# A perceiver block on one core: K and V of all heads first, queries by seven block products, and self scores on 64x64 tiles

## What is computed

```python
def _L0_xattn_ref(q, k, v, Wq, Wk, Wv, Wd):
    queries = (q @ Wq.T).reshape(B, Sq, NHEADS, HEAD_DIM).transpose(0, 2, 1, 3)
    keys = (k @ Wk.T).reshape(B, Skv, KVHEADS, HEAD_DIM).transpose(0, 2, 1, 3)
    values = (v @ Wv.T).reshape(B, Skv, KVHEADS, HEAD_DIM).transpose(0, 2, 1, 3)
    queries = _rope(queries)
    keys = _rope(keys)
    ...
    scores = jnp.einsum('bhqd,bhkd->bhqk', queries, keys) * scale
    scores = jnp.where(causal[None, None], scores, jnp.finfo(scores.dtype).min)
    attn = jax.nn.softmax(scores, axis=-1)
    ctx = jnp.einsum('bhqk,bhkd->bhqd', attn, values)
    ctx = ctx.transpose(0, 2, 1, 3).reshape(B, Sq, NHEADS * HEAD_DIM)
    return ctx @ Wd.T
...
x = x + _L0_xattn_ref(_layernorm(x, axis=-1), ctx_4096, ctx_4096, ...)
x = x + _L0_attn_ref(_layernorm(x, axis=-1), ...)
x = x + _L0_ffn_ref(x, ...)
```

## Time and profile before

| | |
|---|---|
| time, median of 3 runs | 783.68 us (783.64 to 783.75) |
| the profiled execution | 783.46 us, span 781.6 us, the remaining 1.9 us lie outside the span |
| mean granted TensorE clock | 0.985 of full speed |
| first projection matmul | 9.10 us after the span's start |
| first cross scores | 42.49 us |
| last LN transposes ahead of the self attention | 591.48 us |
| end | 781.6 us |

### The profile page before, as it was taken

The page is one execution under the profiler, slowest core; times in us unless marked ns, Lnnn a source line. Parts: engine busy times, 40 slices in busy tenths (PEclk is TensorE's granted clock), DMA queues, the critical chain, the costliest instruction groups (busy, mean ns, idle before and its releaser), DMA issues.

```text
span 781.6 us, 12794 instructions
## 1 busy us (share of the span) xinstructions
PE 757.0 (97%) x4624; PEld 615.4 (79%) x4624; DVE 509.9 (65%) x927; ACT 388.7 (50%) x692; POOL 468.3 (60%) x363
## 2 busy tenths in 40 slices
PE   6989999999999999999999999999799999999898
PEld 4768888888888888888888888888578777777786
DVE  6876565656656565664665656557677777788855
ACT  3557437454553744556274365545436665663220
POOL 4548646764863874686386467646354788864450
PEclk9799999999999999999999999999799999999999
DMA  8102101200210120030021012002002010010002
GB/s 304 55 2 81 55 0 54 81 0 0 85 49 0 55 79 0 24 110 0 0 81 54 0 54 81 0 1 80 3 1 81 14 55 1 2 57 26 14 1 108
DMA packets 11339, 34.11 MB, mean 44 GB/s; under 512 B 1456, under 2 KB 1584, under 8 KB 11312
## 3 DMA queue, kind: packets, MB, share of 16 engines
q1 hardware_dynamic: 11312, 33.75, 13.0%
HBM read 31.65 MB, written 2.10 MB: 43 GB/s over the span
## 4 chain that ended last, share of the span: by engine, by line
PE 86%; DVE 6%; issue 3%; ACT 2%; POOL 2%; DMA 1%; SPq 0%; POOLq 0%; DVEq 0%; ACTq 0%
PE pj L1110 53%; PE pj L1262 8%; PE sc L1142 4%; PE sc L1307 4%; PE pv L1331 2%; PE tp L1320 2%; PE pv L1157 2%; PE pv L1158 2%; PE tp L1150 2%; DVE sm L755 2%; PE pj L1403 1%; PE pj L1466 1%; PE tp L1134 1%; PE pv L1466 1%; PE tp L1466 1%
## 5 line engine op out<-in xcount | busy, mean ns | idle before, releaser
L398 POOL TENSOR_TENSOR sw<-sw,cst 128x512 f32<-128x512 f32 x79 | 109.3, 1383 | 60.7 <-ACT sw L539 60.7
L410 POOL TENSOR_TENSOR sm<-sm,mx 128x512 f32<-128x512 f32 x64 | 67.3, 1051 | 117.8 <-DVE mx L790 117.8
L563 ACT ACTIVATE sm<-sm 128x512 f32<-128x512 f32 x64 | 40.4, 632 | 140.0 <-POOL sm L410 139.7
L538 ACT ACTIVATE sw<-pj 64x512 f32<-64x512 f32 x80 | 47.6, 596 | 118.1 <-DVE t L780 117.7
L1110 PE MATMUL pj<-xh,wqh 128*128 128x512 f32 x252 | 103.4, 410 | 0.2 <-ACT sw L539 0.2
L1110 PE MATMUL pj<-wdh,ch 128*128 128x512 f32 x256 | 101.8, 398 | 0.7 <-ACT sw L539 0.5
L1110 PE MATMUL pj<-wdh,cl 128*128 128x512 f32 x256 | 99.7, 390 | 0.0
L1110 PE MATMUL pj<-wdl,ch 128*128 128x512 f32 x256 | 99.7, 390 | 0.0
L415 POOL TENSOR_TENSOR sm<-sm,rz 128x512 f32<-128x512 f32 x64 | 66.8, 1044 | 54.9 <-DVE rz L797 54.9
L1110 PE MATMUL pj<-xh,wql 128*128 128x512 f32 x252 | 99.7, 395 | 0.0
L1110 PE MATMUL pj<-xl,wqh 128*128 128x512 f32 x252 | 99.3, 394 | 0.0
(11 more groups left out here) (201 smaller groups left out, 1727.7 us busy)
## 6 DMA issues: line engine op xcount, KB each, us to landing
raw<-in_w_x SPq DMA_DIRECT2D x40, 512.0 KB, 3.9
qr<-in_ctxT SPq DMA_DIRECT2D x4, 512.0 KB, 7.1
X<-in_x SPq DMA_DIRECT2D x4, 512.0 KB, 7.3
raw<-in_w_s SPq DMA_DIRECT2D x4, 512.0 KB, 3.6
out<-X SPq DMA_DIRECT2D x8, 256.0 KB, 2.1
raw<-in_w_s SPq DMA_DIRECT2D x4, 256.0 KB, 3.0
raw<-in_w_o SPq DMA_DIRECT2D x2, 512.0 KB, 3.6
raw<-in_w_b SPq DMA_DIRECT2D x2, 512.0 KB, 4.8
```

Of the source, the lines that this page charges most:

```text
L398: pool.tensor_tensor(sw[par][:, :].rearrange("p (b s) -> p b s", s=S), sw[par][:, :].rearrange("p (b s) -> p b s", s=S), rep(cst[:, C_SIN: ...
L410: pool.tensor_tensor(s3, s3, per_group(mx[:, c, :], 8), ALU.subtract).then_inc(subbed, 1)
L538: act.activation(sw[par][0:64, :], src[64:128, :], ACT.Copy)
```

## The change

**K and V first.** All 16 K tiles (`k_tile`, 8 heads by two halves) are computed one after another, in four banks in turn; they go through RoPE and to a DRAM buffer `kscr`. V is computed by token rows, 16 tiles of 128 tokens by 512 channels of four heads (`v_tile`), so it needs no transposes, is copied by ACT and stored in `vscr`. Weights for K and V come in eight pieces through two halves of `raw8`; pieces 0 and 1 are split by POOL, the others by DVE (`piece_lo`). The LN1 transposes (`ln1`) stand behind K tiles 12 to 15 and V tiles 0 to 3. In the head loop SP loads K and V of a head back into single buffers (`load_kr`, `load_vv`).

**Queries by seven block products.** For a pair of query heads the weights are four blocks (two heads by two halves of the 512 channels), and the tokens with their channels four more. Seven products of 6 matmuls each (`product`) replace eight. The sums of the token blocks (`mix`) are made once. Those of the weight blocks (`w7_sum`, four additions of 256 columns from SBUF to SBUF) are made on DVE for each pair in `raw8`, which is single; then ACT makes the high part of the seven blocks (`w7_hi`) and POOL the low part (`w7_lo`, two instructions of 896 columns); `w7` has two buffers. The seven products are accumulated in two banks, A and C. ACT copies partial results out (`part_copy`: `pc`, `u2`), DVE adds them (`c_add`) into `cq` in SBUF, and for three of the four results of a pair the product with the cosines (`t1_mul`) and the swap read `cq` in place of PSUM.

**Softmax and P times V.** The unit is now a head, with four softmax steps. V stays unsplit: `pv_x` is four full-precision fp32 matmuls of 256 columns, each on 64 rows of the array. The probabilities are copied once by ACT. The eight `out_x` of a head are spread between the products of the second pair, most of them in one bank, B.

**Order.** A prelude makes the queries of head 0 in the order `FIRST`; then `head(g, n, more)` runs for heads 0 to 5, once more for head 6 without further weights, and a tail of its own for head 7. Through `x_done`, `out_x(g, j)` waits for the addition of the tile before in the same bank.

**Self scores.** A step is now eight matmuls on 64x64 tiles (rows by columns), and `kb` is half as wide. Both banks of `sc` are used by each step, so scores n wait for mask n-1.

```diff
+            for i in range(2):
+                sp.wait_ge(s_vs[i], 16 * NVT // 2)
+            for i in range(2):
+                load_vv(0, i)
+            for i in range(2):
+                sp.wait_ge(wlo, 4 + 2 * i)
+                load_q(1, i)
...
+            def head(g, last):
+                if not last:
+                    sp.wait_ge(wlo, 4 * g + 8)
+                    load_q(g + 2, 0)
+                sp.wait_ge(scored, 4 * g + 4)
+                load_kr(g + 1)
+                for i in range(2):
+                    sp.wait_ge(wd_lo, 2 * g + 1 + i)
+                    load_d(g + 1, i)
+                sp.wait_ge(pv_t, 4 * g + 2)
+                load_vv(g + 1, 0)
+                if not last:
+                    sp.wait_ge(wlo, 4 * g + 10)
+                    load_q(g + 2, 1)
+                sp.wait_ge(pv_t, 4 * g + 4)
+                load_vv(g + 1, 1)
+
```

```diff
+            def w7_lo(m, p):
+                pool.wait_ge(whi, m + 1)
+                for i in range(2):
+                    c = slice(i * 896, (i + 1) * 896)
+                    pool.tensor_tensor(w7[p][:, 1, c], raw8[:, 1:8, :].rearrange("p n c -> p (n c)")[:, c],
+                                       w7[p][:, 0, c].bitcast(F32), ALU.subtract).then_inc(wlo, 1)
+
...
+                        rope_sin(k % 2, ri(2 * n + p, k))
+                        rope_add(k % 2, ri(2 * n + p, k), q_out(p, k))
+                        if p == 0 and k == 0:
+                            for c in range(2, 4):
+                                normalise(4 * g + c, c)
+                    if more:
+                        w7_lo(2 * n + 2 + p, p)
+
+            with pool.Fori(0, NKV - 2) as g:
+                head(g, g + 1, True)
+            head(NKV - 2, NKV - 1, False)
+
...
+            def w7_hi(m, p, free):
+                act.wait_ge(wsum, 4 * m + 4)
+                if free is not None:
+                    act.wait_ge(stp, free)
+                hi(raw8[:, 1:8, :].rearrange("p n c -> p (n c)"), w7[p][:, 0, :], whi)
```

```diff
+            def t1_k(ki):
+                dve.wait_ge(kproj, ki + 1)
+                if ki >= 2:
+                    dve.wait_ge(rope, ki - 1)
+                dve.tensor_tensor(bs(t1[ki % 2][:, :]), bs(k_bank[ki % 4]), rep(cst[:, C_COS:C_COS + S], HB),
+                                  ALU.mult).then_inc(t1_done, 1)
...
+            def w7_sum(m):
+                dve.wait_ge(s_rq, 16 * (m + 1))
+                a21, a11, a12, a22, b1, b2, b3, b4 = (raw8[:, i, :] for i in range(8))
+                dve.tensor_tensor(b1, a21, a22, ALU.add).then_inc(wsum, 1)
+                dve.tensor_tensor(b3, a11, a21, ALU.subtract).then_inc(wsum, 1)
+                dve.wait_ge(wsum, 4 * m + 1)
+                dve.tensor_tensor(b2, b1, a11, ALU.subtract).then_inc(wsum, 1)
+                dve.wait_ge(wsum, 4 * m + 3)
+                dve.tensor_tensor(b4, a12, b2, ALU.subtract).then_inc(wsum, 1)
+
+            def c_add(par, products, copies, was, bank, copy):
+
+                dve.wait_ge(stp, products)
+                dve.wait_ge(pcp, copies)
+                dve.wait_ge(swp, was)
+                dve.tensor_tensor(cq[par][:, :], bank, copy[:, :], ALU.add).then_inc(cadd, 1)
...
+            piece_lo(7)
+            ln_apply(0)
+            t1_k(12)
+            ln_apply(1)
+            t1_k(13)
+            ln_apply(2)
+            t1_k(14)
+            ln_apply(3)
+            t1_k(15)
+            for n in range(4, NT):
                 ln_apply(n)
```

```diff
+                sum_rec(q + 3, 3)
+                wd_split(g, 1, wdh, wdl)
+                c_lo(q, 0)
+                t1_q(0, 2)
+                c_mix(0, 3)
+                t1_q(0, 3)
+                c_lo(q + 1, 1)
+                if more:
+                    w7_sum(2 * n + 2)
+                out_add(g, 0)
+                out_add(g, 1)
+                c_mix(1, 0)
+                t1_q(1, 0)
+                out_add(g, 2)
+                out_add(g, 3)
+                c_mix(1, 1)
+                t1_q(1, 1)
+                c_lo(q + 2, 2)
+                t1_q(1, 2)
+                c_mix(1, 3)
+                t1_q(1, 3)
...
+                if more:
+                    out_add(g, 5)
+                    out_add(g, 6)
+                    out_add(g, 7)
+
```

```diff
+            def product(bank, p, w, xb, start, stop):
+                for k in range(2):
+                    wh, wl = (w7[p][:, i, w * 256 + k * P:w * 256 + (k + 1) * P] for i in range(2))
+                    mh, ml = (x7[:, xb, i, k * HALF:(k + 1) * HALF] for i in range(2))
+                    for part, (a, r) in enumerate(((wh, mh), (wh, ml), (wl, mh))):
+                        last = pe.matmul(bank, a, r, start=(start and k == 0 and part == 0),
+                                         stop=(stop and k == 1 and part == 2), skip_group_check=True)
+                return last
...
+            def pv_x(g, j):
+                h, c = j // 2, j % 2
+                pe.wait_ge(tp_c, 4 * g + j + 1)
+                if c == 0:
+                    pe.wait_ge(s_vv[h], 16 * (g + 1))
+                if j:
+                    pe.wait_ge(pv_lo, 4 * g + j)
+                for bp in range(2):
+                    for bo in range(2):
+                        rows, cols = slice(64 * bo, 64 * bo + 64), slice(bp * 256, (bp + 1) * 256)
+                        last = pe.matmul(pv[:, bo, cols], vv[rows, 4 * h + 2 * c + bp, :], pt[c][rows, cols],
+                                         start=True, stop=True)
+                last.then_inc(pv_t, 1)
...
+            def head(g, n, more):
+                def free(m):
+                    pe.wait_ge(t1_done, ri(m - 1, 2) + 1)
+                    pe.wait_ge(swp, ri(m - 1, 2) + 1)
+
+                def added(j):
+                    pe.wait_ge(x_done, XD0 + 8 * g + j)
+
+                m = 2 * n
+                pe.wait_ge(rope, ri(m, 0))
+                pe.wait_ge(s_kr, 16 * (g + 1))
+                scores_x(g, 0)
+                scores_x(g, 1)
+                pe.wait_ge(wlo, 2 * m + 2)
+                free(m)
+                product(A_BANK, 0, W_11, X_11, True, False).then_inc(stp, 1)
+                pe.wait_ge(cadd, 3 * m)
+                added(0)
+                product(C_BANK, 0, W_12, X_21, True, True).then_inc(stp, 1)
+                scores_x(g, 2)
+                scores_x(g, 3)
+                pe.wait_ge(cadd, 3 * m + 1)
+                product(A_BANK, 0, W_S2, X_T2, False, False).then_inc(stp, 1)
+                p_transposes(g, 0)
+                product(C_BANK, 0, W_S1, X_T1, True, False).then_inc(stp, 1)
+                pe.wait_ge(pcp, 3 * m + 2)
+                product(A_BANK, 0, W_S3, X_T3, False, False).then_inc(stp, 1)
+                pv_x(g, 0)
+                pe.wait_ge(cadd, 3 * m + 2)
+                product(A_BANK, 0, W_22, X_T4, False, True).then_inc(stp, 1)
+                p_transposes(g, 1)
+                product(C_BANK, 0, W_S4, X_22, False, True).then_inc(stp, 1)
+                pv_x(g, 1)
+                added(-1)
+                out_x(g, 0, B_BANK, wdh, wdl)
+                m = 2 * n + 1
+                pe.wait_ge(wlo, 2 * m + 2)
+                free(m)
+                product(A_BANK, 1, W_11, X_11, True, False).then_inc(stp, 1)
+                added(1)
+                out_x(g, 1, B_BANK, wdh, wdl)
+                pe.wait_ge(cadd, 3 * m)
+                product(C_BANK, 1, W_12, X_21, True, True).then_inc(stp, 1)
+                added(2)
+                out_x(g, 2, B_BANK, wdh, wdl)
+                pe.wait_ge(cadd, 3 * m + 1)
+                product(A_BANK, 1, W_S2, X_T2, False, False).then_inc(stp, 1)
...
-                if n >= 2:
-                    pe.wait_ge(masked, N_SM + n - 1)
+                    pe.wait_ge(pj_act, ST * v + 2)
+                pe.wait_ge(masked, N_SM + n)
                 for b in range(2):
                     bb = 2 * c + b
-                    last = pe.matmul(sc[:, n % 2, b * 256:(b + 1) * 256], qm[h][:, bb, :, :], kb[h][:, bb, :, :],
-                                     start=True, stop=True)
+                    for par in range(2):
+                        for r in range(2):
+                            rows = slice(64 * r, 64 * r + 64)
+                            last = pe.matmul(sc[64 * par:64 * par + 64, r, b * P:(b + 1) * P],
+                                             qm[h][rows, bb, par, :], kb[h][rows, bb, :, :], start=True, stop=True)
```

1577 lines of the change are left out of this document (883 added, 694 removed).

## The result

| | before | after |
|---|---|---|
| time, median | 783.66 us (783.28 to 783.75) | 857.89 us (856.54 to 863.35) |
| ratio, 95% interval | | 1.095 (1.092 to 1.098) |
| profiled execution, its span | 783.46, 781.6 | 856.81, 855.0 |
| mean granted TensorE clock | 0.985 | 0.950 |

The forecast was 835, with a range of 776 to 866. The time lies in the range; the likeliest case was 22 us too low.

A forecast was written before the change was run, and what follows sets the result against it. PE bounds the kernel, busy 757.0 of 781.6 us. Start 168.8, seven heads of 61.3, then -14.1, 2.9, 44.3, 21.4, 190.1 and -9.7 give 832.8 span; plus 1.9 is 835 us, range 776 to 866.

The forecast's parts named there:

- first head's effective start: Prelude: V's end at 121.1 plus 53.8 of RoPE, load and split waits, less 6.05, gives 168.8 us; 42.5 before.
- a steady head: Head loop: 51.7 us of PE work plus waits and a clock fall, 61.3 us a head, before 66.6.
- forecast that L985 to L990 would all be over 1 us: Sign in the new trace: DVE's weight sums in each head take over 1 us each in the mean instead of 0.3.
- First head: Prelude: the fourth weight pair's load waits for POOL's w7_lo(2); the first c_add ends 53.8 us after V.
- The clock: Steady head: the granted clock falls in the 5.7 us idle ahead of the second out_x, costing 1.0 us.
- PE's own work: Steady head: scores, products, out_x, transposes and pv_x sum to 51.7 us, 14.9 less than before.
- Row tiles: Row-tiled matmuls run side by side: pv_x takes 1.0 us and a self scores step 0.59.
- rival 3: Row tiles run one after another: pv_x adds 17 us, self scores 19; 871 us in all, chance 0.10.
- Rivals 1 and 2: Head loop: port waits cost little, 782 us, chance 0.15; or nothing waits inside a head, 762 us, chance 0.11.
- My main case: DVE's two-operand SBUF work waits for POOL's instructions, PE waits behind it: 61.3 us a head, 835 in all, chance 0.62.
- rival 1: Head loop: port waits cost little, POOL being idle when DVE asks; 54.5 us a head, 782 in all, chance 0.15.

The follow-up runs named there:

- e2_filler: Changed kernel plus 18 useless 512-column matmuls per head in PE's gap ahead of the second out_x; 847.2 us.
- e13_last: Kernel of e10_best with the weight sums behind the second pair's first c_add, and ACT's copy of that product ahead of the weights' high part; 771.25 us.
- e9_same: Changed kernel with all four pv_x matmuls on the lower 64 rows, leaving out half of the values; 860.6 us, one execution.
- e11_self: Kernel before the change with only the 64x64 self scores and one mask over both banks; 780.4 us, ratio 0.996.
- e1_sums: Changed kernel with DVE's weight sums behind the first and fifth additions into X instead of ahead; 819.1 us.
- e12_halves: Changed kernel with each POOL RoPE instruction cut in two of 256 columns; 858.6 us.
- e6_ln2: Changed kernel with two LN results behind the fourth K weight piece, the others behind the K tiles, and V's last piece after the sixth; 851.1 us.
- e10_best: Kernel with all earlier moves (793.8 us) plus more reordering in heads, first stage and prelude, including the second addition ahead of the sums; 794.8 us.

## Why the prediction was right, and where it was off

| step | predicted | measured |
|---|---|---|
| idle ahead of the first LN transposes | 12.7 | 13.7 |
| V's last tile ends | 121.1 | 121.9 |
| RoPE results of the first head, behind V | 34.8 | 34.8 (156.7) |
| first head's effective start (measured: end of its first addition into X, 197.5, less the steady 28.1) | 168.8 | 169.4 |
| first addition into X after a head's scores | 28.05 | 28.1 |
| idle ahead of the second output tile, ahead of `out_x` 6 | 5.7, 1.8 | 5.15, 2.02 |
| all idle time of a steady head | 8.6 | 8.6 |
| clock price of the first of these, in the head shown | 1.0 | 3.1 |
| a steady head | 61.3 | 64.7 |
| last head's scores to the last LN transposes | 65.7 | 65.4 |
| from there to the end | 180.4 | 182.4 |
| span | 832.8 | 855.0 |

**The mechanism held.** It was that DVE and POOL, idle 39 and 41% of the span, are late at single places, and PE waits there. Following both engines in their written order through a head gave the time of the first addition within 0.1 us. Part of that is luck: `c_lo` ended 1.1 us later than predicted and the sums took 1.1 less, since only the first two of them meet a POOL instruction. The forecast that L985 to L990 would all be over 1 us is wrong; the groups of lines have 0.84, 1.29, 0.89 and 0.43 in the mean.

**First head.** The wait of the fourth weight pair's load for POOL came as worked out: `w7_lo(2)` ends at 160.8, DVE's sum follows the load at 164.4, and the masks of the first head stand behind it.

```profile
156.68 4.14 POOL L477 TENSOR_TENSOR w<-raw,w 128x896 fp32r<-128x896 f32 x2
...
164.38 0.42 DVE L985 TENSOR_TENSOR raw<-raw 128x256 f32<-128x256 f32 x1 [11.40 <-DMA raw<-in_w_q]
```

**The term that was too small is the head.** Of the 22 us, 20 lie in the seven heads. The measured head is 3.4 us above the forecast, just outside the 3 us that the prediction allowed; the whole stays inside its range of 803 to 862, because the first head's start was right to 1 us. (1) The clock: I took 1.0 us for 5.7 us of idle time. Measured are 5.49 - 2.75 = 2.7 for the twelve matmuls of the second output tile and 0.4 for the product behind them: 3.1 in the head shown. The other loop heads lost about as much, two of them half of it behind the gap of 2.0 us, for which I had taken nothing. e2_filler shows that it is the idle time's price: its heads without the long gap are 2.8 shorter. The row that I had (3.33 for 2.09 after 3.1 us idle) showed the whole price of its gap, for the matmuls behind those scores run at the full distance again. These are the next two of them, and the stretch by stage, both of the kernel before:

```profile
45.75 0.50 PE L1110 MATMUL pj<-ah,wqh 128*128 128x512 f32 x1
46.09 0.39 PE L1110 MATMUL pj<-al,wqh 128*128 128x512 f32 x1
...
42.49:46.00 3.51, 3.51 (x65) 3.44 (x66) 3.47 (x6) 1.06 (x2) 0.00 (x0) 0.60 0.01 2
```

There the low clock lasted about 3 us; behind the 5.15 us it lasted about 6 (worked out from the mean clocks, 0.60 in 3.5 us and 0.57 in 7.2, with 0.5 and 1.0 as the two levels). The price of one gap couldn't be carried over to a longer one. (2) PE's own work: in the window of the head above PE is busy 56.0 us, less the 3.1 of the clock 52.9, not 51.7; in e13_last it is busy 52.6 of 53.3. I had multiplied matmuls by their distance inside a block, but a product of six takes 1.45 to 1.50 from start to start between transposes and scores, for 1.39 by the sum. The waits were right in sum: 8.6 us of idle time a head, as in the forecast (5.7, 1.8 and 1.1 of shorter ones). The 2.1 and 1.2 that were too little are the 3.4 but for rounding.

**Row tiles.** 1.06 for P times V and 0.60 for the self scores, as taken (1.0 and 0.59). e9_same shows that they run side by side, so rival 3 is out by an experiment. The Trainium skill (TensorE: Matmul & The Clock Gate, "Packing small matmuls") agrees: on different rows the step took 1.06, on the same rows 1.92. The sentence of the Trainium skill on draining at a change of tiling mode (TensorEngine Tiling (Array Packing), "Key Properties") fits a small cost at the entry, 0.32 us for 0.24 ahead of the self scores. That is most of the 0.09 by which a step of e11_self saved less than expected; no run here separates it from the cost of other changes.

**Rivals 1 and 2** said that the port costs little, or that nothing waits. A head of 54.5 and one of 51.7 were their numbers. The changed kernel had 64.7, but e13_last reached 53.3 with the same port: what made the head long was what stood behind the instructions that meet the port. My main case had the two as one. The runs separate them in part: e1_sums changed only the place and gained 39 us; e12_halves shortened the single waits at the port and gained nothing in all, but it lengthened POOL's chain too. No run takes the port's waits away with the order as it was, so rival 1's 54.5 for that case is neither shown nor refuted.

**Open.** The 3.4 us that e6_ln2 left ahead of ACT's copy were not removed by themselves. The low clock behind gaps of 2 us came in some heads and not in others that do the same work, and no run shows why. The block products and the new place of K and V weren't run one by one, so what the saved matmuls are worth alone isn't known. The first head's 15 to 19 us of idle time were never removed; they wait for eight RoPE results one by one on POOL, and moving a part of that to DVE or under V's tiles wasn't tried.

## What to carry to other kernels

When a change takes work off the engine that bounds, look in every in-order queue for what stands ahead of the instruction that the bounding engine waits for next: here two groups of four sums of 0.4 us each, put ahead of an addition instead of behind it, cost 39 us in six heads. Put work whose consumer is far away behind work whose consumer is next, and do it again after each step, since the next instruction in line is then the late one (e10_best gained nothing, e13_last, one step further, gained 23.5). An idle gap of the matmul engine can cost more than its length: here 3 us more for 5 us, and 1.6 more for 2 us in two of six heads.

## What the runs showed of the hardware

The low clock outlasts the gap: 5.15 us idle cost 3.1 more behind it in the head shown, 2.0 us idle cost 1.6 more in two heads and nothing in the four others, and in e2_filler, with 18 useless matmuls in the gap, the twelve matmuls behind it ran at the full clock. DVE's LN result (L932), one SBUF operand and two columns of scalars, is slow beside POOL too: 529 ns in the undisturbed group, 1,465 in the mean of another, and 1.52 us at 79.64, where it ended 0.3 after POOL's L465 (79.59, 1.29 us), though I had counted only instructions with two wide operands among those that wait. And four full-precision matmuls on two row groups take 1.06 us whether the groups alternate or not.
